# A two-layer transformer kernel on one core: scratch layout, pipeline distance and start-up order of its first attention are changed

## The chip, the core and the metric

The kernel runs on one core of a Trainium2 chip. Its time is the device time of one execution in microseconds (us). The engines are TensorE (PE, with its weight loads as PEld), VectorE (DVE), ScalarE (ACT), GpSimd (POOL) and SyncE (SP, here used to start transfers); each works through a queue of its own in the order written, and they signal one another with semaphores. 16 DMA engines move data.

## What is computed

Four blocks follow one another on x, 2 x 1024 rows of 128 numbers: an attention with 8 heads, a feed-forward net with ternary weights, a delta-rule attention, a feed-forward net with sign weights. Only the first block is touched by the change:

```
xn = layernorm(x) * gamma + beta
q, k = xn @ Wq + bq, xn @ Wk + bk        # 8 heads of 16 columns
v = xn @ Wv + bv                         # 8 heads of 128 columns
p = softmax(q @ k.T / 4)                 # per batch and head, 1024 x 1024
out = (p @ v).reshape(S, B, D, H).sum(-1)
x = layernorm(x + out)
```

The sum over the last axis adds up 8 neighbouring columns of v, so the kernel sums Wv and bv first, and each head needs 16 columns of v only.

## The kernel before, in words

Two batches of 8 heads are 16 heads, each with 8 tiles of 128 keys or queries.

**Start-up.** The 2048 rows come in four groups of 512 (`GROUPS`). Per group DVE takes statistics (L384), POOL forms the inverse deviation (L297), DVE normalises (L393), PE transposes (L470), ACT applies gamma and beta (L253), PE projects q, k and v (L483, L486, L493), and q and k are cut into a rounded part (ACT, L267, L269) and the rest (DVE, L404, L407). DVE sums Wv and bv (L423, L425) and adds bv to v (L415). `store_splits` (L176) writes the parts to two scratch tensors in DRAM, 3 planes x batch x 128 x 1024, the rounded part twice. `load_stacks` (L187) reads a head back as 48 rows: 3 planes of its 16 rows, each head twice (partitions 0 and 64) for q and for k, four transfers of 192 KB. There are 4 buffers for such stacks. SP does all of it in one order: stores of groups 0 and 1, stacks of head 0, stores of group 2, stacks of head 1, stores of group 3, stacks of head 2, then the ffn weights (L218 to L225, 10 transfers), and only then, head by head, `load_shift(h)` and `load_stacks(h + 3)`; the weights of the third block follow those of heads 0 and 1.

**Steps.** PE then runs through numbered steps (L540). Step s computes the raw scores of one query tile (`row_scores`, L503, L504: head s // 8), DVE takes their row maxima (L446). When a head's 8 maxima are there, POOL splits them (L315), PE transposes them into a row at step 8(h+1)+1 (`shift_step`, L512), ACT copies the row out (L279), and SP lays it into rows 48, 49, 112 and 113 of the head's q stack with four transfers (L203). From step 8(h+1)+5 on (`LAG` = 5, `score_step`) PE computes the transposed scores with the maximum already subtracted (L524), ACT exponentiates them (L285), and 2 steps later PE multiplies with v (L536). So in most steps PE has the row scores of one head, the scores of the head before it, and a product with v. A queue waits as a whole: where L524 of a new head waits for its shift rows, the row scores behind it wait too. At the end of a head DVE folds the result (L453) and POOL adds it to X. A stack buffer is free for head h + 4 when the scores of head h are done (L194). POOL also splits the ffn weights (heads 1 to 6), prepares convolution weights (heads 7 to 9) and masks (head 10).

Of the kernel before, what the change touches and what calls it, by code (L numbers as in the profile page):

```python
# [5 lines left out]
ALU = mybir.AluOpType  # L6
# [41 lines left out]
def build(nc, dr, out_dram):  # L48
    x_dram = dr["L0_attn_x"]
    q_scratch = nc.dram_tensor("q_scratch", (3, B, P, S), F32, kind="Internal").ap()  # L50
    k_scratch = nc.dram_tensor("k_scratch", (3, B, P, S), F32, kind="Internal").ap()

    with ExitStack() as ctx:
        program(nc, dr, out_dram, x_dram, q_scratch, k_scratch, ctx)


def program(nc, dr, out_dram, x_dram, q_scratch, k_scratch, ctx):
# [54 lines left out]
    LAG = 5  # L112
# [5 lines left out]
    wv_sum, bv_sum = sb("wv_sum", [P, P]), sb("bv_sum", [P, P])  # L118
# [5 lines left out]
    wv, bv_rows, ones_row = prob[:, 0, :], prob[:, 1, :], prob[0:2, 2, :]  # L124
# [3 lines left out]
    folded = sb("folded", [P, 2, 8, 32])  # L128
    rsum, att = sb("rsum", [P, 8]), sb("att", [P, 8, DK0])

    with nc.Block() as block:
        x_in = [sem(f"x_in{g}") for g in range(GROUPS)]
        weights_in, v_weights_in = sem("weights_in"), sem("v_weights_in")
# [4 lines left out]
        q_hi, k_hi, q_lo, k_lo, v_ready = sem("q_hi"), sem("k_hi"), sem("q_lo"), sem("k_lo"), sem("v_ready")  # L138
        splits_stored = [sem(f"splits_stored{g}") for g in range(GROUPS)]
# [6 lines left out]
        T_BANK, Q_BANK, K_BANK, V_BANK = 4, 5, 6, 7  # L146
# [7 lines left out]
        def shift_step(h):  # L154
            return 8 * (h + 1) + 1
# [15 lines left out]
        def _(sp):  # L171
# [46 lines left out]
            for o, name in ((W1, "w1"), (W2, "w2")):  # L218
                sp.dma_start(w_raw[:, o:o + FH], dr[f"L0_ffn_{name}_w"]).then_inc(w_in, 16)
            for o, name, n in ((WH1, "h1", FH), (WH2, "h2", FH), (W3, "w3", D)):  # L220
                sp.dma_start(w_raw[:, o:o + FB * n].rearrange("p (k n) -> p k n", k=FB),
                             dr[f"L0_ffn_{name}_w"].rearrange("(k p) n -> p k n", p=P)).then_inc(w_in, 16)
            for i, name in enumerate(("w1", "w2", "h1", "h2")):
                sp.dma_start(ffn_scale[:, i, :], dr[f"L0_ffn_{name}_s"]).then_inc(w_in, 16)
            sp.dma_start(w3s[:], dr["L0_ffn_w3_s"].rearrange("(p o) -> p o", o=1)).then_inc(w_in, 16)  # L225

            for h in range(NH):
# [3 lines left out]
                if h == 0:  # L231
# [3 lines left out]
                if h == 1:  # L235
# [7 lines left out]
        def _(act):  # L243
            for dst, src in ((gam, "gamma"), (bet, "beta"), (bq, "bq"), (bk, "bk")):
                act.dma_start(dst[:], dr["L0_attn_" + src].rearrange("(p o) -> p o", o=1)).then_inc(weights_in, 16)
            for dst, src in ((wq, "Wq"), (wk, "Wk")):
                act.dma_start(dst[:], dr["L0_attn_" + src]).then_inc(weights_in, 16)
# [14 lines left out]
            load_xnT(0)  # L262
            for g in range(GROUPS):
                if g >= 2:
                    act.wait_ge(splits_stored[g - 2], 4 * 16)
                act.wait_ge(q_psum, g + 1)
                nc.scalar.activation(qsp[:, g % 2, 0, :], ps[:, Q_BANK, :], ACT.Identity, bias=bq[:, 0:1]).then_inc(q_hi, 1)  # L267
                act.wait_ge(k_psum, g + 1)
                nc.scalar.activation(ksp[:, g % 2, 0, :], ps[:, K_BANK, :], ACT.Identity, bias=bk[:, 0:1]).then_inc(k_hi, 1)  # L269
                if g + 1 < GROUPS:  # L270
                    load_xnT(g + 1)

            for i, unit in enumerate(ring_order):
# [15 lines left out]
        def _(pool):  # L289
# [17 lines left out]
            nc.gpsimd.memset(vp[:, :, :, 16:17], 1.0).then_inc(ones_set, 1)  # L307
# [56 lines left out]
            for h in range(NH):  # L364
# [16 lines left out]
        def _(dve):  # L381
            link = Chain(dve, dve_step)

            def stats(g):  # L384
# [6 lines left out]
                last.then_inc(stats_ready, 1)  # L391
# [1399 lines left out]
```

## Time and profile before

| | us |
|---|---|
| median of 3 runs (816.42 to 827.82) | 824.22 |
| the profiled execution | 825.39 |
| its span, first to last instruction | 823.7 |
| PE, DVE, ACT, POOL busy | 615.6, 490.4, 284.6, 286.1 |
| mean granted TensorE clock | 0.784 of full |

The busy times are shares of the whole span, in which four blocks with different limits follow one another; they don't tell what bounds the first block. For that one reads its own stretches of time. The granted clock is that of TensorE alone; it has two levels, 1.2 and 2.4 GHz, shown as 0.50 and 1.00.

### The profile page before, as it was taken

The numbers are of one execution on the slowest core, as the hardware profiler recorded it, in microseconds if no ns is written. First come the engines' busy times: TensorE is split into PE (matmuls) and PEld (weight loads), VectorE is DVE, ScalarE is ACT, GpSimd is POOL, SyncE is SP. The second block draws the span as 40 slices with busy tenths as digits, with TensorE's granted clock in tenths as the row PEclk, the third lists the DMA queues.
The fourth block names the chain that finished last, engine by engine and source line by source line (L and its number), as shares of the span: only waits on it lengthen the run. The fifth ranks groups of instructions, "written<-read, shape, count | busy, mean of one in ns | idle before, by whom it ended". The sixth has DMA issues, their size and how long they took to land. (4 is left out here: it accounts for less than half of the span.)

```text
span 823.7 us, 16498 instructions
## 1 busy us (share of the span) xinstructions
PE 615.6 (75%) x6944; PEld 378.0 (46%) x6944; DVE 490.4 (60%) x790; ACT 284.6 (35%) x519; POOL 286.1 (35%) x385
## 2 busy tenths in 40 slices
PE   4440898988999896999998588859733489448884
PEld 2210333333333334777676366644423378335662
DVE  5460588678568524554545323347997897655773
ACT  2200566567457463243341144520100011214331
POOL 2100142324201012554455302489960002236673
PEclk9855689799558577999999889988956555558887
DMA  4645311111111000000000010102202000000000
GB/s 134 227 162 151 106 53 65 62 65 56 45 49 60 4 2 2 1 0 1 1 0 1 0 28 2 26 30 53 53 3 53 4 4 3 2 0 1 13 14 25
DMA packets 36910, 32.18 MB, mean 39 GB/s; under 512 B 21588, under 2 KB 28244, under 8 KB 36836
## 3 DMA queue, kind: packets, MB, share of 16 engines
q1 hardware_dynamic: 35684, 29.94, 12.0%
q10 hardware_dynamic: 1152, 1.18, 0.5%
q8 instruction: 55, 0.90, 0.5%
q14 instruction: 19, 0.16, 0.1%
HBM read 21.35 MB, written 9.44 MB: 37 GB/s over the span
## 5 line engine op out<-in xcount | busy, mean ns | idle before, releaser
L446 DVE TENSOR_REDUCE nmx<-ps 128x1 f32<-128x1024 f32 x128 | 154.6, 1221 | 100.3 <-PE ps L504 99.7
L285 ACT ACTIVATE prob<-ps 128x512 f32<-128x512 f32 x256 | 136.9, 596 | 109.0 <-PE ps L524 106.7
L524 PE MATMUL ps<-qst,kst 50*128 50x512 f32 x256 | 87.8, 600 | 41.8 <-DMA qst<-shift_sb 40.1
L536 PE MATMUL ps<-prob,vp 128*32 128x256 f32 x1024 | 99.3, 481 | 0.0
L633 POOL TENSOR_TENSOR h_lo<-hf,h_hi 128x512 fp32r<-128x512 f32 x48 | 63.7, 1338 | 69.6 <-DVE h_hi L663 69.6
L524 PEld LDWEIGHTS ps<-qst,kst 50*128 50x128 f32 x256 | 35.3, 223 | 107.3 <-ACT prob L285 46.3
L503 PE MATMUL ps<-kst,qst 48*128 48x512 f32 x128 | 67.4, 530 | 22.8 <-DMA kst<-k_scratch 18.9
L315 POOL CAST nsplit<-nmx 128x8 fp32r<-128x8 f32 x16 | 3.0, 190 | 214.7 <-DVE nmx L446 202.7
L504 PE MATMUL ps<-kst,qst 48*128 48x512 f32 x128 | 65.7, 516 | 0.0
L663 DVE CAST h_hi<-hf 128x512 fp32r<-128x512 f32 x48 | 41.8, 897 | 37.9 <-ACT hf L606 37.3
L707 PE MATMUL ps<-h_hi,w_lo 128*128 128x512 f32 x144 | 58.5, 406 | 7.7 <-issue 5.4
L1037 DVE SCALAR_TENSOR_TENSOR long_<-vpad,fir_l,long_ 128x1024 f32<-128x1024 f32 x46 | 59.0, 1285 | 1.5
L708 PE MATMUL ps<-h_lo,w_hi 128*128 128x512 f32 x144 | 57.0, 395 | 0.0
L709 PE MATMUL ps<-h_hi,w_hi 128*128 128x512 f32 x144 | 56.8, 395 | 0.0
L1663 POOL TENSOR_TENSOR h_lo<-hf,h_hi 128x512 fp32r<-128x512 f32 x32 | 43.7, 1390 | 23.4 <-DVE h_hi L1689 23.4
L536 PEld LDWEIGHTS ps<-prob,vp 128*32 128x32 f32 x1024 | 24.7, 122 | 55.3 <-issue 32.8
L503 PEld LDWEIGHTS ps<-kst,qst 48*128 48x128 f32 x128 | 31.3, 246 | 28.4 <-DMA kst<-k_scratch 19.6
L1689 DVE CAST h_hi<-hf 128x512 fp32r<-128x512 f32 x32 | 34.9, 1144 | 15.3 <-ACT hf L1633 15.0
L606 ACT ACTIVATE hf<-ps,ffn_scale 128x512 f32<-128x512 f32 x32 | 22.1, 690 | 59.1 <-PE ps L709 58.8
L707 PEld LDWEIGHTS ps<-h_hi,w_lo 128*128 128x128 f32 x144 | 27.0, 188 | 19.8 <-issue 8.7
L1227 POOL TENSOR_TENSOR vtok<-vtok,sq 128x512 f32<-128x512 f32 x4 | 5.1, 1263 | 86.6 <-DVE sq L1109 86.6
L504 PEld LDWEIGHTS ps<-kst,qst 48*128 48x128 f32 x128 | 31.6, 248 | 0.0
(236 smaller groups left out, 1187.4 us busy)
## 6 DMA issues: line engine op xcount, KB each, us to landing
qst<-q_scratch SPq DMA_DIRECT2D x32, 192.0 KB
kst<-k_scratch SPq DMA_DIRECT2D x32, 192.0 KB
q_scratch<-qsp SPq DMA_DIRECT2D x4, 512.0 KB, 3.3
k_scratch<-ksp SPq DMA_DIRECT2D x4, 512.0 KB, 4.4
w_raw<-L_ffn_h_w SPq DMA_DIRECT2D x2, 1024.0 KB, 13.2
X<-L_attn_x SPq DMA_DIRECT2D x4, 256.0 KB, 4.8
q_scratch<-qsp SPq DMA_DIRECT2D x4, 256.0 KB, 4.2
k_scratch<-ksp SPq DMA_DIRECT2D x4, 256.0 KB, 8.6
```

Source lines behind the costliest of these rows:

```text
L285: nc.scalar.activation(prob[:, n % PROBS, GT * half:GT * half + GT], ps[:, RINGB + i % RING, :], ACT.Exp, scale=SCORE_SCALE).then_inc(ring ...
L446: nc.vector.tensor_reduce(nmx[:, h % 2, k:k + 1], pair, AX.X, ALU.max, negate=True).then_inc(max_done, 1)
L503: nc.tensor.matmul(ps[:, bank, :], qst[0:48, p, P * k:P * k + P], kst[0:48, p, 0:GT], start=True, stop=True)
L504: nc.tensor.matmul(ps[:, bank + 1, :], qst[64:112, p, P * k:P * k + P], kst[64:112, p, GT:S], start=True, stop=True).then_inc(max_psum, 1)
L524: nc.tensor.matmul(ps[:, RINGB + i % RING, :], kst[r:r + 50, p, P * t:P * t + P], qst[r:r + 50, p, GT * half:GT * half + GT], start=True, ...
L536: last = nc.tensor.matmul(ps[32 * j:32 * j + 32, PVB, 0:256], vp[:, h, t, :], prob[:, n % PROBS, 256 * j:256 * j + 256], start=(t == 0), s ...
L633: nc.gpsimd.tensor_tensor(h_lo[:, layer % 2, o, :], hf[:, o, :], h_hi[:, layer % 2, o, :].bitcast(F32), ALU.subtract).then_inc(lo_ready, 1)
L707: nc.tensor.matmul(out, wl, xh, start=start, stop=False)
L708: nc.tensor.matmul(out, wh, xl, start=False, stop=False)
L709: return nc.tensor.matmul(out, wh, xh, start=False, stop=stop)
L1037: ins = nc.vector.scalar_tensor_tensor(long_[:, b], vpad[:, b, t:t + S], fir_l[:, t:t + 1], long_[:, b], ALU.mult, ALU.add)
L1663: nc.gpsimd.tensor_tensor(h_lo[:, layer, o, :], hf[:, o, :], h_hi[:, layer, o, :].bitcast(F32), ALU.subtract).then_inc(lo_ready, 1)
```

## The change

The scratch tensors become batch x 128 x 3 x 1024, so that the 48 rows of a head lie one behind the other, and the loads of a head read them as such. The rows of heads 0 and 1 (the first 32) are stored first. Stacks of heads 0 to 2 are loaded before the stores of groups 2 and 3. The shift goes in with two transfers rather than four and one step later (+2); the scores follow at +8 rather than +5, so 6 steps lie between the two rather than 4. The ffn weights are started after head 1's shift and stacks, those of the third block after heads 3 and 4, and POOL's work on them moves by three heads. In the start-up q and k of groups 0 and 1 get PSUM banks of their own, ACT copies v out, POOL sums Wv and bv by halves, bv enters by a matmul with a row of ones, DVE waits for the four small vectors first and adds the epsilon, and the projections of group 3 are done in steps 1 to 3. PE gets 12 extra matmuls at the start and 2 in each of the steps 5 to 17, whose results nobody reads.

```diff
-    q_scratch = nc.dram_tensor("q_scratch", (3, B, P, S), F32, kind="Internal").ap()
-    k_scratch = nc.dram_tensor("k_scratch", (3, B, P, S), F32, kind="Internal").ap()
+    q_scratch = nc.dram_tensor("q_scratch", (B, P, 3, S), F32, kind="Internal").ap()
+    k_scratch = nc.dram_tensor("k_scratch", (B, P, 3, S), F32, kind="Internal").ap()
...
-    LAG = 5
+    LAG = 8
...
-T_BANK, Q_BANK, K_BANK, V_BANK = 4, 5, 6, 7
+T_BANK, V_BANK = 4, 7
+Q_BANK, K_BANK = (0, 2, 5, 5), (1, 3, 6, 6)
+EARLY = 2 * DK0
...
-    return 8 * (h + 1) + 1
+    return 8 * (h + 1) + 2
...
-    def store_splits(g):
+    def store_rows(g, rows, done):
         b, cols = g // 2, slice(GT * (g % 2), GT * (g % 2) + GT)
-        q_rows = q_scratch[:, b, :, cols].rearrange("a p t -> p a t")
-        k_rows = k_scratch[:, b, :, cols].rearrange("a p t -> p a t")
...
         sp.wait_ge(q_lo, g + 1)
-        sp.dma_start(q_rows[:, 0:2], qsp[:, g % 2].bitcast(F32)).then_inc(splits_stored[g], 16)
-        sp.dma_start(q_rows[:, 2:3], qsp[:, g % 2, 0:1].bitcast(F32)).then_inc(splits_stored[g], 16)
+        sp.dma_start(q_rows[:, 0:2], qsp[rows, g % 2].bitcast(F32)).then_inc(done, 16)
+        sp.dma_start(q_rows[:, 2:3], qsp[rows, g % 2, 0:1].bitcast(F32)).then_inc(done, 16)
         sp.wait_ge(k_lo, g + 1)
-        sp.dma_start(k_rows[:, 1:3], ksp[:, g % 2].bitcast(F32)).then_inc(splits_stored[g], 16)
-        sp.dma_start(k_rows[:, 0:1], ksp[:, g % 2, 0:1].bitcast(F32)).then_inc(splits_stored[g], 16)
+        sp.dma_start(k_rows[:, 1:3], ksp[rows, g % 2].bitcast(F32)).then_inc(done, 16)
+        sp.dma_start(k_rows[:, 0:1], ksp[rows, g % 2, 0:1].bitcast(F32)).then_inc(done, 16)
...
-        if h % 8 == 0:
+        if h == 0:
+            sp.wait_ge(first_rows_stored, 2 * 4 * 16)
+        if h == 2 or h == 8:
             sp.wait_ge(splits_stored[2 * b], 4 * 16)
             sp.wait_ge(splits_stored[2 * b + 1], 4 * 16)
...
-            sp.dma_start(qst[r:r + 48, p, :].bitcast(F32), q_scratch[:, b, rows, :]).then_inc(stack_in[p], 16)
-            sp.dma_start(kst[r:r + 48, p, :].bitcast(F32), k_scratch[:, b, rows, :]).then_inc(stack_in[p], 16)
+            sp.dma_start(qst[r:r + 48, p, :].bitcast(F32), q_scratch[b, rows].rearrange("e a t -> (e a) t")).then_inc(stack_in[p], 16)
+            sp.dma_start(kst[r:r + 48, p, :].bitcast(F32), k_scratch[b, rows].rearrange("e a t -> (e a) t")).then_inc(stack_in[p], 16)

     def load_shift(h):
         sp.wait_ge(ring_done, ring["shift", h] + 1)
         for r in (48, 112):
-            for j in range(2):
-                sp.dma_start(qst[r + j:r + j + 1, h % STACKS, :].bitcast(F32),
-                             shift_sb[8 * j:8 * j + 8, h % 2, :].bitcast(F32)).then_inc(shift_in, 16)
...
+            sp.dma_start(qst[r:r + 2, h % STACKS, :].bitcast(F32), shift_sb[:, h % 2, :].bitcast(F32)).then_inc(shift_in, 16)
+
+    sp.dma_start(wv, dr["L0_attn_Wv"]).then_inc(v_weights_in, 16)
+    sp.dma_start(bv_row, dr["L0_attn_bv"].rearrange("(o n) -> o n", o=1)).then_inc(v_weights_in, 16)
...
-    store_splits(0)
-    store_splits(1)
+    early_rows, other_rows, all_rows = slice(0, EARLY), slice(EARLY, P), slice(0, P)
+    store_rows(0, early_rows, first_rows_stored)
+    store_rows(1, early_rows, first_rows_stored)
     load_stacks(0)
-    store_splits(2)
+    store_rows(0, other_rows, splits_stored[0])
+    store_rows(1, other_rows, splits_stored[1])
     load_stacks(1)
-    store_splits(3)
     load_stacks(2)
-
...
+    store_rows(2, all_rows, splits_stored[2])
+    store_rows(3, all_rows, splits_stored[3])
+
+    def load_ffn_weights():
...
-        if h == 0:
+        if h == 1:
+            load_ffn_weights()
+        if h == 3:
...
-        if h == 1:
+        if h == 4:
...
-    act.dma_start(wv, dr["L0_attn_Wv"]).then_inc(v_weights_in, 16)
-    act.dma_start(bv_rows, dr["L0_attn_bv"].rearrange("(o n) -> o n", o=1).broadcast_to([P, H0 * D])).then_inc(v_weights_in, 16)
+        act.dma_start(dst[:], dr["L0_attn_" + src]).then_inc(qk_weights_in, 16)
...
-    act.wait_ge(weights_in, 6 * 16)
+    act.wait_ge(ln_weights_in, 4 * 16)
...
+    def leading_q(g):
         if g >= 2:
             act.wait_ge(splits_stored[g - 2], 4 * 16)
+            act.wait_ge(first_rows_stored, 2 * 4 * 16)
         act.wait_ge(q_psum, g + 1)
-        nc.scalar.activation(qsp[:, g % 2, 0, :], ps[:, Q_BANK, :], ACT.Identity, bias=bq[:, 0:1]).then_inc(q_hi, 1)
+        nc.scalar.activation(qsp[:, g % 2, 0, :], ps[:, Q_BANK[g], :], ACT.Identity, bias=bq[:, 0:1]).then_inc(q_hi, 1)
+
+    def leading_k(g):
         act.wait_ge(k_psum, g + 1)
-        nc.scalar.activation(ksp[:, g % 2, 0, :], ps[:, K_BANK, :], ACT.Identity, bias=bk[:, 0:1]).then_inc(k_hi, 1)
-        if g + 1 < GROUPS:
-            load_xnT(g + 1)
+        nc.scalar.activation(ksp[:, g % 2, 0, :], ps[:, K_BANK[g], :], ACT.Identity, bias=bk[:, 0:1]).then_inc(k_hi, 1)
...
+    def values(g):
+        b, half = g // 2, g % 2
+        act.wait_ge(v_psum, g + 1)
+        nc.scalar.copy(vp[:, 8 * b:8 * b + 8, 4 * half:4 * half + 4, 0:DK0],
+                       ps[:, V_BANK, :].rearrange("p (t h e) -> p h t e", t=4, e=DK0)).then_inc(v_ready, 1)
+
+    load_xnT(0)
+    leading_q(0)
+    load_xnT(1)
+    leading_k(0)
+    leading_q(1)
+    leading_k(1)
+    values(0)
+    load_xnT(2)
+    values(1)
+    load_xnT(3)
+    leading_q(2)
+    leading_k(2)
+    values(2)
+    leading_q(3)
+    leading_k(3)
+    values(3)
...
-        link(nc.gpsimd.tensor_scalar(rs[:, g, :], mv[:, g, :, 1], LN_EPS, None, ALU.add))
...
+    pool.wait_ge(v_weights_in, 2 * 16)
+    for src, dst in ((wv, wv_sum), (bv_row, bv_sum)):
+        n8 = src.rearrange("p (n e) -> p n e", e=H0)
+        link(nc.gpsimd.tensor_tensor(n8[:, :, 0:4], n8[:, :, 0:4], n8[:, :, 4:8], ALU.add))
+        link(nc.gpsimd.tensor_tensor(n8[:, :, 0:2], n8[:, :, 0:2], n8[:, :, 2:4], ALU.add))
+        nc.gpsimd.tensor_tensor(dst[:].rearrange("p (n o) -> p n o", o=1), n8[:, :, 0:1], n8[:, :, 1:2], ALU.add).then_inc(wv_summed, 1)
...
-        if 1 <= h < 7:
-            if h == 1:
+        if 4 <= h < 10:
+            if h == 4:
                 pool.wait_ge(w_in, 16 * W_LOADS)
-            for i in range(2 * h - 2, min(2 * h, WSPLITS)):
+            for i in range(2 * h - 8, min(2 * h - 6, WSPLITS)):
                 split_weights(i)
-        if 7 <= h < 10:
-            convolve_weights(h - 7)
-        if h == 10:
+        if 10 <= h < 13:
+            convolve_weights(h - 10)
+        if h == 13:
             make_masks()
...
-        last.then_inc(stats_ready, 1)
+        link(last)
+        nc.vector.tensor_scalar(rs[:, g, :], mv[:, g, :, 1], LN_EPS, None, ALU.add).then_inc(stats_ready, 1)
...
+    dve.wait_ge(ln_weights_in, 4 * 16)
     stats(0)
     stats(1)
     normalise(0)
-    dve.wait_ge(v_weights_in, 2 * 16)
-    nc.vector.tensor_reduce(wv_sum[:], wv.rearrange("p (n e) -> p n e", e=H0), AX.X, ALU.add).then_inc(wv_summed, 1)
     normalise(1)
-    nc.vector.tensor_reduce(bv_sum[:], bv_rows.rearrange("p (n e) -> p n e", e=H0), AX.X, ALU.add).then_inc(wv_summed, 1)
     stats(2)
-    left_over(0)
+    rest_q(0)
+    rest_k(0)
     stats(3)
+    rest_q(1)
+    rest_k(1)
     normalise(2)
-    dve.wait_ge(wv_summed, 2)
-    values(0)
-    left_over(1)
     normalise(3)
-    values(1)
-    left_over(2)
-    values(2)
-    left_over(3)
-    values(3)
+    rest_q(2)
+    rest_k(2)
...
+        if step == 3:
+            rest_q(3)
+            rest_k(3)
...
+    def warm(columns, count):
+        for _ in range(count):
+            nc.tensor.matmul(ps[:, V_BANK, 0:P], columns, ident[:], start=True, stop=True)
...
+    def project_q(g):
+        if g == 0:
+            pe.wait_ge(qk_weights_in, 2 * 16)
+        pe.wait_ge(xnT_ready, g + 1)
+        if g == 3:
+            pe.wait_ge(q_lo, g)
+        nc.tensor.matmul(ps[:, Q_BANK[g], :], wq[:], xnT[:, g % 2, :], start=True, stop=True).then_inc(q_psum, 1)
+
+    def project_k(g):
+        if g == 3:
+            pe.wait_ge(k_lo, g)
+        nc.tensor.matmul(ps[:, K_BANK[g], :], wk[:], xnT[:, g % 2, :], start=True, stop=True).then_inc(k_psum, 1)
...
+    def project_v(g):
+        if g == 0:
+            pe.wait_ge(wv_summed, 2)
+            pe.wait_ge(ones_set, 2)
+        else:
+            pe.wait_ge(v_ready, g)
+        for n in range(4):
+            out = ps[:, V_BANK, P * n:P * n + P]
+            nc.tensor.matmul(out, xnT[:, g % 2, P * n:P * n + P], wv_sum[:], start=True, stop=False)
+            last = nc.tensor.matmul(out, one[:], bv_sum[:], start=False, stop=True)
+        last.then_inc(v_psum, 1)
+
+    warm(ident[:], 12)
     transposes(0)
...
+    project_q(0)
+    transposes(1)
+    project_k(0)
+    project_q(1)
+    project_k(1)
+    project_v(0)
+    transposes(2)
+    project_v(1)
+    project_q(2)
+    project_k(2)
+    transposes(3)
+    project_v(2)
...
+        if step == 0:
+            pe.wait_ge(q_lo, 2)
+            pe.wait_ge(k_lo, 2)
...
+        if step == 1:
+            project_q(3)
+        if step == 2:
+            project_k(3)
+        if step == 3:
+            project_v(3)
+        if step == 5:
+            pe.wait_ge(v_ready, GROUPS)
+        if 5 <= step < shift_step(0) + LAG:
+            for _ in range(2):
+                nc.tensor.matmul(ps[:, PVB, 256:256 + P], wq[:], ident[:], start=True, stop=True)
```

## Rows read from the trace of the kernel before

**Rows 1.** Windows by stage: busy us (and instructions) per engine, clock, DMA share, GB/s.

```profile
43.07:82.92 39.85, 9.90 (x27) 3.69 (x28) 14.89 (x13) 0.26 (x1) 0.39 (x2) 0.50 0.52 159
82.92:313.46 230.54, 209.11 (x1525) 78.99 (x1525) 148.09 (x146) 140.26 (x271) 53.10 (x119) 0.77 0.15 51
```

**Rows 2.** Timeline of the start-up: start us, duration us, engine, line, instruction, idle before.

```profile
10.74 2.08 PE L483 MATMUL ps<-xnT,wq 128*128 128x512 f32 x2 [1.21 <-ACT xnT L258]
...
22.66 0.75 DVE L407 SCALAR_TENSOR_TENSOR ksp<-ps,bk,ksp 128x512 fp32r<-128x512 f32 x1
...
23.20 1.02 PE L483 MATMUL ps<-xnT,wq 128*128 128x512 f32 x2
...
24.59 0.71 SPq L185 DMA_DIRECT2D k_scratch<-ksp  x1
...
29.32 0.76 SPq L196 DMA_DIRECT2D qst<-q_scratch  x1
...
43.08 0.79 PE L503 MATMUL ps<-kst,qst 48*128 48x512 f32 x1 [13.67 <-DMA kst<-k_scratch]
...
43.91 9.14 DVE L446 TENSOR_REDUCE nmx<-ps 128x1 f32<-128x1024 f32 x8 [11.73 <-PE ps L504]
```

**Rows 3.** Windows, columns as in rows 1: group stores; ffn weights; stack loads alone.

```profile
21.62:25.03 3.41, 3.19 (x17) 1.97 (x16) 3.41 (x13) 1.90 (x3) 2.35 (x5) 1.00 0.96 354
...
62.58:72.82 10.24, 0.00 (x0) 0.00 (x0) 0.89 (x1) 0.00 (x0) 0.00 (x0) 0.50 0.87 227
243.49:246.90 3.41, 3.41 (x17) 1.36 (x17) 2.10 (x5) 1.67 (x4) 0.00 (x0) 0.50 0.20 67
```

**Rows 4.** Timeline: head 0's shift row copied, and SP's last weight transfer.

```profile
58.45 0.26 ACT L279 CAST shift_sb<-ps 16x128 fp32r<-16x128 f32 x1 [27.92 <-PE ps L512]
...
76.56 0.69 SPq L225 DMA_DIRECT2D w3s<-L_ffn_w_s  x1
```

**Rows 5.** Waits: engine, line, what it waited for: us in total, times, longest.

```profile
PE ps L524 <- DMA qst<-shift_sb: 40.1, 12, 20.9
```

**Rows 6.** Timeline of two shifts, behind a stack load and without one.

```profile
191.95 0.73 SPq L196 DMA_DIRECT2D qst<-q_scratch  x1
...
200.28 2.71 SPq L203 DMA_DIRECT2D qst<-shift_sb  x4
...
206.62 0.50 PE L524 MATMUL ps<-qst,kst 50*128 50x512 f32 x2 [2.73 <-DMA qst<-shift_sb]
...
252.82 2.71 SPq L203 DMA_DIRECT2D qst<-shift_sb  x4
...
256.71 0.49 PE L524 MATMUL ps<-qst,kst 50*128 50x512 f32 x2 [0.49 <-DMA qst<-shift_sb]
```

**Rows 7.** Windows, columns as in rows 1: a shift wait, and what followed.

```profile
202.53:205.94 3.41, 1.36 (x16) 0.46 (x12) 2.05 (x2) 1.52 (x3) 0.95 (x1) 1.00 0.20 66
...
209.36:250.31 40.95, 40.95 (x228) 14.66 (x222) 24.65 (x25) 20.12 (x39) 6.93 (x31) 0.50 0.13 47
```

**Rows 8.** Timeline of SP: shifts of neighbouring heads, at full and at half clock.

```profile
110.03 2.70 SPq L203 DMA_DIRECT2D qst<-shift_sb  x4
...
121.06 2.71 SPq L203 DMA_DIRECT2D qst<-shift_sb  x4
...
217.31 2.71 SPq L203 DMA_DIRECT2D qst<-shift_sb  x4
...
235.08 2.71 SPq L203 DMA_DIRECT2D qst<-shift_sb  x4
```

**Rows 9.** Timeline of PE: first and last scores of the last head.

```profile
302.67 0.49 PE L524 MATMUL ps<-qst,kst 50*128 50x512 f32 x2 [0.23 <-DMA qst<-shift_sb]
...
310.64 0.68 PE L524 MATMUL ps<-qst,kst 50*128 50x512 f32 x2
```

**Rows 10.** DMA issues: transfer, queue, count, KB, us to landing.

```profile
bk<-L_attn_bk ACTq DMA_DIRECT2D x1, 0.5 KB, 4.9
```

**Rows 11.** Timeline of PE: the v projection of a group, 4 matmuls in 8 records.

```profile
25.37 1.13 PE L493 MATMUL ps<-wv_sum,xnT 128*128 128x128 f32 x8
```

More of the change, by code:

```diff
@@ L128, in program @@
     folded = sb("folded", [P, 2, 8, 32])
+    one = sb("one", [1, P])
     rsum, att = sb("rsum", [P, 8]), sb("att", [P, 8, DK0])
@@ L208, in _ @@
                 sp.dma_start(kst[r:r + 2, :, :].bitcast(F32), ones_row.rearrange("p (o t) -> p o t", o=1).broadcast_to([2, STACKS, S])).then_inc(ones_in, 16)
-            store_splits(0)
-            store_splits(1)
+            early_rows, other_rows, all_rows = slice(0, EARLY), slice(EARLY, P), slice(0, P)
+            store_rows(0, early_rows, first_rows_stored)
+            store_rows(1, early_rows, first_rows_stored)
             load_stacks(0)
-            store_splits(2)
+            store_rows(0, other_rows, splits_stored[0])
+            store_rows(1, other_rows, splits_stored[1])
             load_stacks(1)
-            store_splits(3)
             load_stacks(2)
[L218 to L225, printed above, removed]
+            store_rows(2, all_rows, splits_stored[2])
+            store_rows(3, all_rows, splits_stored[3])
+            def load_ffn_weights():
+                for o, name in ((W1, "w1"), (W2, "w2")):
+                    sp.dma_start(w_raw[:, o:o + FH], dr[f"L0_ffn_{name}_w"]).then_inc(w_in, 16)
+                for o, name, n in ((WH1, "h1", FH), (WH2, "h2", FH), (W3, "w3", D)):
+                    sp.dma_start(w_raw[:, o:o + FB * n].rearrange("p (k n) -> p k n", k=FB),
+                                 dr[f"L0_ffn_{name}_w"].rearrange("(k p) n -> p k n", p=P)).then_inc(w_in, 16)
+                for i, name in enumerate(("w1", "w2", "h1", "h2")):
+                    sp.dma_start(ffn_scale[:, i, :], dr[f"L0_ffn_{name}_s"]).then_inc(w_in, 16)
+                sp.dma_start(w3s[:], dr["L0_ffn_w3_s"].rearrange("(p o) -> p o", o=1)).then_inc(w_in, 16)
             for h in range(NH):
@@ L295, in _ @@
             link(nc.gpsimd.memset(neg_half[:], -0.5))
+            nc.gpsimd.memset(one[:], 1.0).then_inc(ones_set, 1)
             def rstd(g):
                 pool.wait_ge(stats_ready, g + 1)
-                link(nc.gpsimd.tensor_scalar(rs[:, g, :], mv[:, g, :, 1], LN_EPS, None, ALU.add))
                 nc.gpsimd.tensor_tensor(rs[:, g, :], rs[:, g, :], neg_half[:, 0:4], ALU.pow).then_inc(rstd_ready, 1)
@@ L400, in normalise, with rest_q, rest_k @@
                 last.then_inc(xn_ready, 1)
-            def left_over(g):
+            def rest_q(g):
                 dve.wait_ge(q_hi, g + 1)
-                nc.vector.scalar_tensor_tensor(qsp[:, g % 2, 1, :], ps[:, Q_BANK, :], bq[:, 0:1], qsp[:, g % 2, 0, :].bitcast(F32),
+                nc.vector.scalar_tensor_tensor(qsp[:, g % 2, 1, :], ps[:, Q_BANK[g], :], bq[:, 0:1], qsp[:, g % 2, 0, :].bitcast(F32),
                                                ALU.add, ALU.subtract).then_inc(q_lo, 1)
+            def rest_k(g):
                 dve.wait_ge(k_hi, g + 1)
-                nc.vector.scalar_tensor_tensor(ksp[:, g % 2, 1, :], ps[:, K_BANK, :], bk[:, 0:1], ksp[:, g % 2, 0, :].bitcast(F32),
+                nc.vector.scalar_tensor_tensor(ksp[:, g % 2, 1, :], ps[:, K_BANK[g], :], bk[:, 0:1], ksp[:, g % 2, 0, :].bitcast(F32),
                                                ALU.add, ALU.subtract).then_inc(k_lo, 1)
-            def values(g):
-                b, half = g // 2, g % 2
-                dve.wait_ge(v_psum, g + 1)
-                heads = vp[:, 8 * b:8 * b + 8, 4 * half:4 * half + 4, 0:16].rearrange("p h t e -> p t h e")
-                for t in range(4):
-                    last = nc.vector.tensor_tensor(heads[:, t], ps[:, V_BANK, 128 * t:128 * t + 128].rearrange("p (h e) -> p h e", e=16),
-                                                   bv_sum[:].rearrange("p (h e) -> p h e", e=16), ALU.add)
-                last.then_inc(v_ready, 1)
+            dve.wait_ge(ln_weights_in, 4 * 16)
             stats(0)
@@ L476, in transposes @@
                 last.then_inc(xnT_psum, 1)
-            transposes(0)
-            for g in range(GROUPS):
+            def project_q(g):
+                if g == 0:
+                    pe.wait_ge(qk_weights_in, 2 * 16)
                 pe.wait_ge(xnT_ready, g + 1)
-                if g >= 1:
+                if g == 3:
                     pe.wait_ge(q_lo, g)
-                nc.tensor.matmul(ps[:, Q_BANK, :], wq[:], xnT[:, g % 2, :], start=True, stop=True).then_inc(q_psum, 1)
-                if g >= 1:
+                nc.tensor.matmul(ps[:, Q_BANK[g], :], wq[:], xnT[:, g % 2, :], start=True, stop=True).then_inc(q_psum, 1)
+            def project_k(g):
+                if g == 3:
                     pe.wait_ge(k_lo, g)
-                nc.tensor.matmul(ps[:, K_BANK, :], wk[:], xnT[:, g % 2, :], start=True, stop=True).then_inc(k_psum, 1)
-                if g + 1 < GROUPS:
-                    transposes(g + 1)
-                pe.wait_ge(wv_summed, 2)
-                if g >= 1:
+                nc.tensor.matmul(ps[:, K_BANK[g], :], wk[:], xnT[:, g % 2, :], start=True, stop=True).then_inc(k_psum, 1)
[4 more added lines that the diff above has]
+                else:
                     pe.wait_ge(v_ready, g)
                 for n in range(4):
-                    last = nc.tensor.matmul(ps[:, V_BANK, P * n:P * n + P], xnT[:, g % 2, P * n:P * n + P], wv_sum[:], start=True, stop=True)
+                    out = ps[:, V_BANK, P * n:P * n + P]
+                    nc.tensor.matmul(out, xnT[:, g % 2, P * n:P * n + P], wv_sum[:], start=True, stop=False)
+                    last = nc.tensor.matmul(out, one[:], bv_sum[:], start=False, stop=True)
                 last.then_inc(v_psum, 1)
+            warm(ident[:], 12)
+            transposes(0)
+            project_q(0)
[10 more added lines that the diff above has]
+            project_v(2)
             def row_scores(h, k):
```

22 lines of the change are left out of this document (10 added, 12 removed).

## The prediction

> **What bounds the kernel now.** I read the windows by stage first, then the timeline of what ends the waits in each. Nothing of the change reaches past the first attention, which ends at 313.46 us [rows 1], so the other 510 us are carried over as they are. The attention has two stretches. Until 82.92 almost nothing runs: between 43.07 and 82.92 PE is busy 9.90 of 39.85 us [rows 1]. From 82.92 on PE is busy 209 of 230.5 us, against 148 for DVE, 140 for ACT and 53 for POOL [rows 1]. So PE bounds the second stretch, but at a mean clock of 0.77, and not without holes.
>
> Three things stand behind these numbers, and the reader should see each in its row.
>
> *Narrow loads.* While only stacks are loaded, the DMA engines are busy 0.20 of the time and move 67 GB/s; group stores and ffn weights reach shares of 0.96 and 0.87, and 354 and 227 GB/s [rows 3]. 0.20 is about 3 of 16 engines, and the source of a stack load has 3 planes as its outermost dimension where the stores have 128 rows. A head's four transfers (0.79 MB) take 0.79/67 = 11.7 us at that rate; the first row scores wait 13.8 us from the first issue of head 0's load, 29.32 to 43.08 [rows 2].
>
> *Late shifts.* Head 0's shift row is copied at 58.45, but SP starts its last weight transfer at 76.56 and only then turns to it [rows 4]: the longest wait, 20.9 us. The other 11 waits for shift rows sum to 40.1 - 20.9 = 19.2 us [rows 5]. With no stack load ahead, a shift needs 3.9 us from first issue to scores (252.82 to 256.71); behind one it needs 6.3 (200.28 to 206.62, with the stack load issued from 191.95 on) [rows 6].
>
> *Low clock.* A stretch with such a wait, PE busy 1.36 of 3.41 us, is followed by 41 us at 0.50 (1.2 GHz), with PE recorded busy throughout, 40.95 of 40.95 [rows 7]. A head takes 121.06 - 110.03 = 11.03 us at full clock and 235.08 - 217.31 = 17.77 us at half [rows 8], so each us at half clock costs 1 - 11.03/17.77 = 0.38 us. A mean of 0.77 over 230.5 us is 2 x 0.23 x 230.5 = 106 us at half, a loss of 40 us.
>
> Check: step 13 to step 127 is 114 steps of 11.03/8 = 1.38 us, or 157; then 15 steps at the pace of the last head's scores, (310.64 - 302.67)/7 = 1.14 [rows 9], or 17; 157 + 17 + 19 + 40 = 233, against 230.5 recorded.
>
> **The start-up, to the first row maxima.** DVE now waits for four small vectors, the last of which needs 4.9 us to land [rows 10] and is there some 7 us in, about 3 us after DVE started before. Against that, PE no longer waits between projections for DVE, sums of Wv are POOL's (two trees of three small additions, done by about 16 us, before PE asks for them), and values are ACT's. What counts is the last split of group 1, 23.41 us before [rows 2]. Four projections of q and k at 2 us each (early pace) or 1 (later pace) [rows 2] set it: 20 to 25; I take 22. Then: stores of 32 rows, two k issues and landing, 4 us (before, with 128 rows, 4.7 from 24.59 to 29.32 [rows 2]), so head 0's loads are issued from 26; four issues of 0.73 to 29; four stores of the other rows, 2.4, and 4 to land, 35.3; these gate ACT's rounded q of group 2, whose buffer they empty; with three operations of 0.75 the DVE queue gets to its first maximum at 37.6, against 43.91 [rows 2]. The stacks themselves are there by 32: at 227 to 354 GB/s they need 2.2 to 3.5 us rather than 11.7. Heads 1 and 2 are loaded behind this and have 8 and 16 steps of cover.
>
> **Steps 0 to 15.** Their floor is DVE's 9.14/8 = 1.14 us per maximum [rows 2], 18.3 us. Group 3's projections now stand in steps 1 to 3: q and k 2 us each at half clock, v twice a group's 1.13 [rows 11] because of the ones row, 4.5 at half; 8.5 in all, about 6 beyond what DVE hides (2 at full clock). The two extra matmuls per step cost 0.28 each (1.13/4), 0.56 at half; DVE's maximum covers them at full clock, at half the cover is gone for about 0.4 us a step, and six such steps give 2.5. The 12 at the start fill time in which PE has nothing. First scores at 37.6 + 18.3 + 6 + 2.5 = 64.4 (57 to 70), against 82.92. Head 0's shift is ready at step 10 and has six steps; no weights stand in front of it.
>
> **The pipeline after it.** 111 steps of 1.38 lead to step 127: 153 us. Moving scores from +5 to +8 lengthens the tail to 18 steps of 1.14, 20.5 us, and 0.5 for the last fold: end at 238.4 if the clock stays up and nothing waits, 75 us before 313.46. Of that 75, about 18.5 is the earlier start, 19 the shift waits, 40 the low clock; the three later steps give back 3.
>
> The shift waits go for three reasons: stack loads leave the queues within about 3.5 us, the shift has two issues (1.35 us) instead of four (2.71), and six steps (8.3 us) between its transpose and its use instead of four. One margin shrinks: stacks of head h + 3 are now issued at step 8h + 15 and needed at 8h + 24, 9 steps rather than 12, 12.4 us; issue and landing need 2.9 + about 2, and SP is free again 0.9 us before the next shift. POOL's weight work moves by three heads; with 53 us of work in 230 it stays far from the path, and a shift split queues behind one head's share at most, which the two extra steps cover.
>
> The ffn weights now stand on SP between head 4's stacks and head 2's shift. 5632 columns x 128 x 4 bytes are 2.88 MB: 8.1 to 12.7 us at 354 to 227 GB/s [rows 3]. Shift 2 adds 2.5 to be issued and land: 10.6 to 15.2, against 12.4 - 2.9 = 9.5 us of cover. PE waits 1 to 6 us there; I take 3. The later block's weights (1 MB, heads 3 and 4) stay within the cover.
>
> The clock is what I can't compute. It will be low at the first steps, where PE has had nothing to do; one low stretch of the trace lasts 41 us with PE busy throughout [rows 7], and the wait at head 2 can begin another. Between none and two such stretches I take half of one, 21 us at half beyond step 16: 8 us.
>
> **Sum.** Span 823.7 - 75 + 3 + 8 = 759.7; the profiled execution took 825.39, 1.7 more than its span and 1.2 above the median. Forecast: 761 us. Its own range: 746 to 778.
>
> **Rivals.** About 2% (16.5 us: 807.7 and 840.7) is what a measurement tells from no change.
>
> *The clock comes back at once,* and no wait takes it down: 761 - 8 = 753. For it: the loss of the clock in [rows 7] follows a wait of PE, and these go. Against it: the 41 us in the second of those rows. The Trainium skill, "TensorE: Matmul & The Clock Gate", Part 1, says that sustained matmul work releases the clock soon, and that only idleness takes it back; the first half of that disagrees with the 41 us of [rows 7], the second agrees. By that rule the result would be this rival's.
>
> *Long low stretches stay,* about 100 us as now, begun by the start-up or the weights wait: 761 + (100 - 21) x 0.38 = 791.
>
> *The loads stay narrow,* that is, the layout does not do what it is for: then a load needs 11.7 + 2 us against 12.4 of cover, the next shift stands behind it as before, the stores of the other rows land behind head 0's stacks and the maxima start at 44 as before, first scores at 71, and the pipeline keeps its 230.5 + 3: end at 305, 820 in all with the weights wait. Against it: the 128-row transfers of [rows 3]. The Trainium skill, "DMA: Bandwidth & Descriptors", section on why a DMA increments its semaphore by 16, says that the number of engines is the largest divisor, up to 16, common to both sides' outermost dimensions. By it a stack load goes from 3 to 16 engines, as 0.20 agrees for the 3; by it a shift transfer, 2 rows outermost, goes onto 2 engines. No row shows that; a late shift would show it.
>
> *Slower:* in the first steps the clock stays low and never returns, since a stream at half clock already feeds on itself for 41 us in [rows 7]. Step pace 2.22, tail 1.84 a step: first scores 67, 111 x 2.22 = 247, tail 33, end at 347, 859 in all. It decides for slower only once over (840.7 - 753)/0.38 = 231 of those 280 us are at half; before it was 106 of 230.
>
> **Chances.** Forecast 0.62, clock at once 0.12, long low stretches 0.14, narrow loads 0.07, low throughout 0.03, something unseen 0.02. Faster 0.90, within 2% 0.07, slower 0.03. The range goes from 743 (first scores at 57, no half clock, 1 us at the weights) to 795 (first scores at 70, 75 us at half, 6 us at the weights, and most of the third case).
>
> **What would show it.** Stack loads at a DMA share near 0.9 for some 3 us; first row maxima near 38 and first scores near 64; shift waits gone but for one of 1 to 6 us at head 2; heads 11.0 us apart; last fold near 249; a mean clock over 0.9 in the pipeline. The prediction is wrong if the shift waits remain, if PE stays at half for over 75 us, or if another engine sets the pace of a head.

## The result, and the profile after

The changed kernel takes 769.2 us (median of 4 runs, 758.2 to 778.8) against 826.0 for the kernel before: 0.926 of it, 95% interval 0.907 to 0.945. The forecast was 761 with a range of 743 to 795. The profiled execution took 765.9 us, its span is 764.2. All ratios and intervals here compare only the fast executions of both kernels (those within about 1.5% of their kernel's fastest), while the medians are over all of them, so that a ratio is not the quotient of two medians.

The windows by stage and of single events, with the columns of [rows 1], cut at the first scores (72.46) and the last fold (257.59), which stood at 82.92 and 313.46:

```profile
38.84:72.46 33.62, 33.62 (x98) 19.62 (x97) 20.47 (x18) 2.80 (x5) 0.39 (x2) 0.50 0.55 150
72.46:257.59 185.13, 174.49 (x1528) 67.47 (x1527) 144.64 (x144) 139.91 (x271) 53.82 (x119) 0.94 0.34 75
101.30:108.20 6.90, 2.10 (x12) 0.70 (x12) 0.83 (x1) 1.09 (x2) 0.00 (x0) 0.65 0.69 137
108.20:253.50 145.30, 141.84 (x1297) 54.34 (x1293) 123.14 (x124) 118.44 (x230) 51.79 (x111) 0.99 0.31 64
150.60:152.40 1.80, 1.80 (x22) 0.67 (x16) 1.79 (x2) 1.65 (x4) 0.40 (x2) 1.00 0.64 184
150.28:153.50 3.22, 3.22 (x36) 1.14 (x34) 3.17 (x4) 2.91 (x6) 0.40 (x2) 1.00 0.71 163
257.59:764.17 506.58, 376.32 (x5328) 282.66 (x5328) 309.19 (x558) 134.46 (x234) 223.82 (x244) 0.81 0.06 13
```

The pipeline lasts 185 us where it lasted 230.5. DVE and ACT do the same work as in [rows 1]; what shrinks is PE's idle time, from 21.4 to 10.6 us, and its time at half clock: the mean clock went from 0.77 to 0.94. From 108 to 253 us the clock is 0.99 of full and PE is busy 142 of 145 us. While SP issues a stack load (fifth row), the DMA share is now 0.64 at 184 GB/s, and over 3.2 us from the first issue (sixth row) 0.71 at 163 GB/s, where [rows 3] had 0.20 and 67; the forecast was a share near 0.9.

The waits of PE for shift rows (columns of [rows 5]); there were 12 of 40.1 us:

```profile
PE ps L581 <- DMA qst<-shift_sb: 6.4, 1, 6.4
```

Its place, in the timeline of SP and PE:

```profile
88.16 0.31 SPq L201 DMA_DIRECT2D qst<-q_scratch  x1
...
89.92 0.90 SPq L228 DMA_DIRECT2D w_raw<-L_ffn_w_w  x2
...
92.63 3.93 SPq L233 DMA_DIRECT2D ffn_scale<-L_ffn_w_s  x2
...
97.95 1.47 SPq L234 DMA_DIRECT2D w3s<-L_ffn_w_s  x1
99.46 1.27 SPq L207 DMA_DIRECT2D qst<-shift_sb  x2
...
106.10 0.79 PE L581 MATMUL ps<-qst,kst 50*128 50x512 f32 x2 [6.42 <-DMA qst<-shift_sb]
```

Head 4's stacks, ffn weights, and then head 2's shift: SP gets to the shift 9.5 us after the first weight transfer, and its rows are there another 6.6 us later, behind the 2.88 MB. The start-up, to be held against [rows 2]:

```profile
28.52 0.80 PE L534 MATMUL ps<-wv_sum,xnT 128*128 128x128 f32 x2
29.24 0.79 PE L535 MATMUL ps<-bv_sum,one 1*128 1x128 f32 x2
...
35.48 0.39 PE L534 MATMUL ps<-wv_sum,xnT 128*128 128x128 f32 x2
...
35.68 0.78 ACT L267 ACTIVATE xnT<-ps,bet,gam 128x512 f32<-128x512 f32 x1 [3.58 <-PE ps L510]
36.36 0.68 ACT L276 ACTIVATE qsp<-ps,bq 128x512 fp32r<-128x512 f32 x1
...
38.84 0.79 PE L560 MATMUL ps<-kst,qst 48*128 48x512 f32 x1
...
39.67 2.36 DVE L474 TENSOR_REDUCE nmx<-ps 128x1 f32<-128x1024 f32 x2 [1.19 <-PE ps L561]
```

And two of the steps 5 to 15, in PE's timeline, with the shifts of neighbouring heads later on, in SP's:

```profile
65.70 1.22 PE L620 MATMUL ps<-ident,wq 128*128 128x128 f32 x4
66.85 0.79 PE L560 MATMUL ps<-kst,qst 48*128 48x512 f32 x1
...
67.58 1.22 PE L620 MATMUL ps<-ident,wq 128*128 128x128 f32 x4
```

```profile
155.20 1.27 SPq L207 DMA_DIRECT2D qst<-shift_sb  x2
...
165.97 1.27 SPq L207 DMA_DIRECT2D qst<-shift_sb  x2
```

A step lasts 67.58 - 65.70 = 1.88 us there, and the first row maximum is at 39.67. A head takes 165.97 - 155.20 = 10.77 us at full clock.

### The profile page after: what moved, and what is told of

The parts are those of the page before. It is cut to its first block and busy times, and to the rows that moved or that the text cites. A ratio compares the mean times of both kernels' runs of the same rounds, so it can differ in the third digit from the quotient of the medians.

```text
span 764.2 us, 16680 instructions
## 1 busy us (share of the span) xinstructions
PE 614.1 (80%) x7052; PEld 389.6 (51%) x7052; DVE 491.6 (64%) x776; ACT 286.6 (38%) x523; POOL 290.7 (38%) x388
## 5 line engine op out<-in xcount | busy, mean ns | idle before, releaser
L581 PE MATMUL ps<-qst,kst 50*128 50x512 f32 x256 | 75.3, 516 | 10.0 <-DMA qst<-shift_sb 6.4
L593 PE MATMUL ps<-prob,vp 128*32 128x256 f32 x1024 | 80.8, 401 | 0.0
L581 PEld LDWEIGHTS ps<-qst,kst 50*128 50x128 f32 x256 | 28.7, 189 | 65.6 <-ACT prob L317 43.6
L560 PE MATMUL ps<-kst,qst 48*128 48x512 f32 x128 | 59.6, 468 | 0.0
L561 PE MATMUL ps<-kst,qst 48*128 48x512 f32 x128 | 58.1, 457 | 0.0
L593 PEld LDWEIGHTS ps<-prob,vp 128*32 128x32 f32 x1024 | 22.2, 110 | 44.1 <-ACT prob L317 32.0
L1758 DVE CAST h_hi<-hf 128x512 fp32r<-128x512 f32 x32 | 35.0, 1145 | 13.9 <-ACT hf L1702 13.1
L1702 ACT ACTIVATE hf<-ps,s_out 128x512 f32<-128x512 f32 x32 | 20.7, 689 | 29.4 <-PE ps L1814 18.6
L778 PEld LDWEIGHTS ps<-h_hi,w_hi 128*128 128x128 f32 x144 | 27.0, 188 | 6.6
```

The source lines that it names most:

```text
L560: nc.tensor.matmul(ps[:, bank, :], qst[0:48, p, P * k:P * k + P], kst[0:48, p, 0:GT], start=True, stop=True)
L561: nc.tensor.matmul(ps[:, bank + 1, :], qst[64:112, p, P * k:P * k + P], kst[64:112, p, GT:S], start=True, stop=True).then_inc(max_psum, 1)
L581: nc.tensor.matmul(ps[:, RINGB + i % RING, :], kst[r:r + 50, p, P * t:P * t + P], qst[r:r + 50, p, GT * half:GT * half + GT], start=True, ...
L593: last = nc.tensor.matmul(ps[32 * j:32 * j + 32, PVB, 0:256], vp[:, h, t, :], prob[:, n % PROBS, 256 * j:256 * j + 256], start=(t == 0), s ...
L778: return nc.tensor.matmul(out, wh, xh, start=False, stop=stop)
```

## Experiments

The open questions: which part of the change brings the gain, whether narrow loads, late shifts and low clock are one chain, and what the new wait and the slow first steps cost. The theory: the width of the stack loads is nearly all of it. The rival: distance, order and start-up carry a good part. Medians of this table come from 4 to 6 runs (7 or 11 for the kernel before); first scores, last fold, waits and half clock are of the one profiled execution of each (half clock from first scores to last fold, from the granted clock).

| kernel | median us | ratio to before (95%) | first scores | last fold | shift waits us | at half us |
|---|---|---|---|---|---|---|
| before | 824 to 833 | 1 | 82.9 | 313.5 | 40.1 | 108 |
| changed | 769.2 | 0.926 (0.907 to 0.945) | 72.5 | 257.6 | 6.4 | 21 |
| layout only | 755.5 | 0.916 (0.910 to 0.922) | 60.7 | 250.5 | 16.0 | 38 |
| changed, old layout | 819.9 | 0.980 (0.970 to 0.990) | 76.7 | 326.3 | 24.0 | 150 |
| changed, weights early | 758.0 | 0.917 (0.910 to 0.924) | 72.2 | 248.0 | 0 | 11 |
| changed, no extra matmuls | 765.3 | 0.925 (0.917 to 0.933) | 64.0 | 251.7 | 6.1 | 33 |
| changed, old distance | 766.4 | 0.937 (0.924 to 0.949) | 67.9 | 264.4 | 9.3 | 43 |
| both repairs | 747.5 | 0.916 (0.910 to 0.923) | 62.4 | 235.6 | 4.7 | 9 |
| all, weights spread | 749.9 | 0.914 (0.906 to 0.923) | 58.2 | 233.6 | 0 | 13 |
| layout and spread | 743.2 | 0.912 (0.904 to 0.920) | 50.7 | 233.5 | 5.9 | 20 |
| the same, two transfers | 743.0 | 0.902 (0.890 to 0.913) | 50.0 | 229.6 | 0.2 | 26 |

The kernel before was run beside each group of kernels, at 827.0, 824.8 and 833.2 us. The rows stand by group: layout only to no extra matmuls; old distance, both repairs, layout and spread; the other two.

**Layout only.**

```diff
-q_scratch = nc.dram_tensor("q_scratch", (3, B, P, S), ...)
+q_scratch = nc.dram_tensor("q_scratch", (B, P, 3, S), ...)
-sp.dma_start(qst[r:r + 48, p, :]..., q_scratch[:, b, rows, :])
+sp.dma_start(qst[r:r + 48, p, :]..., q_scratch[b, rows].rearrange("e a t -> (e a) t"))
```

(The same for k, and for the views that the stores write through.)

> The kernel before with the new scratch layout and the loads that read it, nothing else. Theory (the width of the stack loads is the cause of nearly all of it): a stack load lasts about 3 us on all DMA engines, row maxima begin near 34 us, SP is through with the ffn weights near 60, first scores at 62 to 66 instead of 82.9; a shift needs 3.9 us and has four steps of 1.38, so the 11 short shift waits go and with them most of the half clock; 755 to 775 us. Rival (distance, order and start-up carry a good part): shift waits of 1 to 3 us stay at the heads, 785 to 805 us.

755.5 us: the layout alone gives the whole gain. Its median is 14 us below that of the full change, but the two intervals, 0.910 to 0.922 and 0.907 to 0.945, overlap: that it is faster is not shown. Windows of it, the start-up's DMA (stores of group 3 and stacks together) and the pipeline's last 154 us; then its waits, all and between 96 and 250 us; then head 0's shift:

```profile
36.00:40.00 4.00, 2.43 (x8) 0.86 (x6) 4.00 (x4) 0.00 (x0) 0.00 (x0) 0.50 1.07 326
...
96.30:249.90 153.60, 146.12 (x1335) 57.86 (x1335) 125.44 (x127) 121.09 (x235) 44.23 (x105) 0.99 0.28 56
```

```profile
PE ps L524 <- DMA qst<-shift_sb: 16.0, 14, 11.5
...
PE ps L524 <- DMA qst<-shift_sb: 4.6, 13, 1.0
```

```profile
46.28 0.26 ACT L279 CAST shift_sb<-ps 16x128 fp32r<-16x128 f32 x1 [16.32 <-PE ps L512]
...
53.93 2.72 SPq L203 DMA_DIRECT2D qst<-shift_sb  x4
...
60.69 0.79 PE L524 MATMUL ps<-qst,kst 50*128 50x512 f32 x2 [11.45 <-DMA qst<-shift_sb]
```

With the old distance and four transfers, 13 shifts cost 4.6 us (0.35 each, at most 1.0) instead of 19.2 us in 11, and once the clock has risen at 98.4 it stays until after the last fold. Head 0's shift still waits behind the block of weights: its row is there at 46.54, and SP turns to it at 53.93. The first row maximum comes at 35.85, against 43.91 in the kernel before and 39.67 in the changed one.

**Changed, old layout.** The layout's edit undone, all others kept.

> The changed kernel with the old scratch layout (three planes outermost) and all its other edits. Theory: DMA share near 0.2 while stacks load, a load of 11.7 us, shift waits of 1 to 4 us at most heads and low clock after them, 805 to 825 us. Rival (the greater distance and the two transfers are enough): few waits, at most 785 us.

As the theory said, 819.9; at 0.970 to 0.990, the other edits without the layout bring 1 to 3%. What the theory had not said: the greater distance does take most of the waits away, 4 are left. Windows at one of them and behind it:

```profile
144.09:150.91 6.82, 1.61 (x20) 0.46 (x12) 2.29 (x2) 1.76 (x4) 0.39 (x2) 0.80 0.22 74
154.33:195.28 40.95, 40.95 (x219) 14.22 (x222) 23.77 (x25) 20.80 (x41) 11.82 (x20) 0.50 0.13 47
```

Of PE's 150 us at half clock here, 20 lie before the first wait; the other 130 are four stretches, one begun at each of the four waits (13.1, 6.2, 2.2 and 2.5 us long). The profiled execution, 837 us, is longer than the kernel's median. So a wait of a few us costs itself and then the low stretch behind it: the one of these windows lasts from 148.1 to 199.3, the one of [rows 7] from 208.0 to 252.3. The short waits are another matter: no wait of the kernel before under 1.9 us, and none of the 13 of the layout alone behind 96 us, the longest of 1.0, is followed by a fall of the clock, while in the kernel before five of the six from 1.96 to 3.4 us are. The first row maximum is at 44.64 here, no earlier than the 43.91 of before.

**Changed, weights early.** `load_ffn_weights()` stands before the loop over heads, as in the kernel before.

> The changed kernel with the ffn weights started before head 0's shift again, as in the kernel before. Theory (the move is not needed once stack loads are fast, and costs a wait at head 2): SP is through with them near 62, just before shift 0 is ready at 63; the wait of 6.4 us at head 2 and the 7 us of half clock around it go: 7 to 9 us less, 755 to 763 us. Rival (they delay shift 0): first scores 5 to 20 us later, 770 to 790 us.

No shift wait is left and the last fold comes 9.5 us earlier; the median, 758.0 us, is 11 below that of the changed kernel, though the intervals overlap. With wide loads SP is through with the weights at 58.2, before shift 0 is ready at 63.2. By the profiles the move of the weights was a cost, not a gain.

**Changed, no extra matmuls.**

```diff
-if 5 <= step < shift_step(0) + LAG:
-    for _ in range(2):
-        nc.tensor.matmul(ps[:, PVB, 256:256 + P], wq[:], ident[:], start=True, stop=True)
```

> The changed kernel without the two extra matmuls in steps 5 to 17 (the 12 at the start stay). Theory (they are on the path at half clock): these steps take 1.14 us instead of 1.87, first scores near 64 instead of 72.5, 757 to 764 us. Rival (they bring the clock back early and are worth their cost): first scores near 64, but PE stays at half 20 to 40 us longer, 768 to 778 us.

The row maxima behind group 3's projections, in DVE's timeline:

```profile
51.95 14.80 DVE L474 TENSOR_REDUCE nmx<-ps 128x1 f32<-128x1024 f32 x13 [3.97 <-PE ps L561]
```

They follow one another without a gap at 14.80/13 = 1.14 us, though PE is at half clock, and first scores come at 64.0, as expected, 8.5 us earlier. The total, 765.3, is just above the expected 757 to 764, and its interval overlaps that of the changed kernel: in the profiled execution the wait at head 2 brought 24 us at half instead of 7. Alone, this run settles the cost of the extra matmuls in their steps, not in the total. Nothing shows that they bring the clock back: PE is at full clock 8.9 us after first scores without them (at 72.9) and 13.8 with them (at 86.3); with the weights early it is 8.7 without (both repairs) and 11.3 with. In the other kernels without them it is 9 to 38.

**Changed, old distance.** `LAG` = 5, shift at +1, four transfers.

> The changed kernel with the distance of before (shift at +1, scores at +5) and four shift transfers again. Theory (with wide stack loads a shift needs 3.9 us and four steps of 1.38 hold it nearly): first scores after 13 steps, some 6 us earlier, short waits of at most 1 us per head, 4 to 6 us in all; about the same as the changed kernel, 760 to 772 us, the one long wait now at head 1 or 2, where the ffn weights stand. Rival (the greater distance is needed): waits of 1 to 3 us at each head and low clock after them, 780 to 800 us.

766.4 us, inside the theory's 760 to 772. First scores come 4.6 us earlier; 13 waits cost 9.3 us rather than the expected 4 to 6, 5.5 of it at the weights, where 34 us at half clock begin. Six steps or four is worth nothing that this can measure.

**Both repairs.** Weights early and no extra matmuls.

> The changed kernel with the ffn weights back in their old place and without the extra matmuls in steps 5 to 17: both repairs at once. Theory (both costs are on the path and add): first scores near 64, no wait at head 2, last fold at 238 to 246, 745 to 756 us. Rival (without the extra matmuls the clock stays low longer): last fold at 248 to 256, 757 to 766 us.

747.5 us, last fold at 235.6, before the expected 238 to 246: 22 us earlier than in the changed kernel, where the two repairs alone gave 9.5 and 5.9, so the two costs add. Some 2 us of the rest are chance: up to the first row maximum the code is that of the changed kernel, and the maximum came at 37.72 here, at 39.34 to 39.67 with the one repair, the other or none. A wait of 4.7 us stays at head 0: its shift row is copied by 52.7 now, and SP is at the weights until 57.1. **No bias rows** is the same, but leaves bv out, and so computes another result:

> As the run with both repairs, and bv left out (the matmul with the row of ones is not issued), to price it. Theory (group 1's and 2's v projections at half clock hold up the last rounded parts, and so the first row maximum): first maximum at 34 to 37 us instead of 39.6. Rival (the stores of the other rows set it, as I had predicted): it stays within 0.5 us of 39.6.

One run, 744.2 us. The first maximum is at 36.30, against 37.72 with both repairs. ACT's rounded q of group 2 is released by the landing of the stores in either, first with both repairs, then without bias rows:

```profile
35.68 0.69 ACT L276 ACTIVATE qsp<-ps,bq 128x512 fp32r<-128x512 f32 x1 [0.75 <-DMA k_scratch<-ksp]
...
34.26 0.69 ACT L276 ACTIVATE qsp<-ps,bq 128x512 fp32r<-128x512 f32 x1 [4.53 <-DMA k_scratch<-ksp]
```

So the stores are the gate that I had predicted, in both, and the 1.4 us between the two are a difference in when the stores landed: they don't price the ones row, and the theory of this run, that PE's v projections held up the rounded parts, is not shown by it. In the profiled execution of the changed kernel PE did come last.

**Layout and spread.** The kernel before, new layout, and the ffn weights behind the stacks of heads 0 to 3:

```diff
 load_stacks(h + 3)
+load_ffn_weights(h)   # h = 0: w1, w2; 1: h1; 2: h2; 3: w3 and the scales
```

> The kernel before with the new layout, and its ffn weights spread over heads 0 to 3, one or two transfers behind each head's stacks (POOL's splits three heads later, as in the changed kernel). Theory (the weights in one block were the 11.5 us wait at head 0 of the run with the layout alone): first scores near 50 instead of 60.7, no wait over 1.5 us, last fold at 236 to 244, 742 to 754 us. Rival (each part of the weights delays the next shift instead, or the low clock lasts as much longer): 755 to 765 us.

743.2 us, first scores at 50.7, last fold at 233.5 (expected 236 to 244): the best so far, and none of the start-up's reordering is in it. The first row maximum is at 35.96. **All, weights spread** is the changed kernel without its extra matmuls and with this spread:

> The changed kernel without the extra matmuls in steps 5 to 17 and with the ffn weights spread over heads 0 to 3. Theory (the start-up order, the stores and the distance bring little of their own): first scores near 58, some 7 us later than in the kernel with the layout and the spread weights alone, but no shift waits: last fold at 229 to 236, 738 to 750 us, within 1% of that one. Rival (order and distance are worth something once the waits are gone): 5 to 10 us faster than it, 733 to 738 us.

749.9: first scores 7.6 us later, no waits, the same last fold (233.6 against 233.5). The first row maximum is at 38.39, 2.4 us later, for all the reordering before it. The rest of the change is worth nothing here. What each part of the reordered start-up does alone (the early stores, the banks, the matmul for bv) was not tested. **The same, two transfers** puts the shift's two transfers into the kernel with layout and spread:

> The kernel with the new layout and the spread weights, and the shift in two transfers instead of four, at the old distance. Theory (half the issue time, 1.3 us less before the shift has landed): the 15 waits of 5.9 us in all go to under 1 us, 739 to 744 us. Rival (a transfer of two rows lands later, being carried by fewer DMA engines): waits as long or longer, 743 to 750 us.

The waits go from 5.9 us to 0.2, so a transfer of two rows does not land late enough to be waited for; the total, 743.0, does not move by what can be measured. The two kernels ran in different groups; 733.3 to 748.9 and 741.5 to 749.7 overlap.

## Why the prediction was right, point by point

*Loads.* Right, and shown both ways: the layout alone gives 0.916, all the rest without it 0.980. The Trainium skill, "DMA: Bandwidth & Descriptors", section on why a DMA increments its semaphore by 16, would give 3 engines for three planes outermost and 16 for 48 rows; the 0.20 of [rows 3] and the 0.22 above agree with the first, and the shares of 0.64 and 0.71 with more than 3. Its 2 engines for the new shift transfers may hold, but cost nothing that shows.

*Late shifts.* Right for the 11 waits. The wait at head 2 was predicted at 1 to 6 us, taken as 3, and is 6.4. The term that was short is landing: the shift's rows need 6.6 us from first issue behind the weights, not the 2.5 taken from a queue without them.

*Pipeline.* From first scores to last fold 174 + 3 + 8 = 185 us were forecast and 185.1 measured. That is partly luck. The wait was 3.4 us longer than taken, and a head took 10.77 us rather than 11.03, which gives back 3.6 over the 111 steps. Half clock was taken as 21 us there and is 21, but between 9 and 43 in the experiments with wide loads: the 21 was a middle.

*Clock.* The rival in which it comes back at once (753) did not come: PE was at half from 38.5 to 86.3. The step behind the forecast, that the clock falls where PE waits, holds for the fall at head 2 (103.4, in the wait of 6.4 us). It is not the whole: in the start-up the clock fell at 38.5 with no wait of PE before it (rows at the end). With this fall the sentence that only idleness takes the clock back, which the prediction found borne out by [rows 7], does not agree.

*Steps 0 to 15.* Here the prediction failed: first scores at 72.5, outside the 57 to 70 given. The step that failed is "at half the cover is gone for about 0.4 us a step, and six such steps give 2.5". The price of the two matmuls was right: 1.15 us from start to start (65.70 to 66.85), where 1.12 was taken. But with the row scores' 0.73 behind them (66.85 to 67.58) a step of PE is 1.88 us, 0.74 above DVE's 1.14 rather than 0.4; the 0.79 of a row score at half clock in [rows 2] would have given 0.79 + 1.12 - 1.14 = 0.77. And PE stayed at half in all 11 of these steps before the first scores, not in six: 8.1 us in place of 2.5. The rest of the term held: without the extra matmuls 37.6 + 18.3 + 6 = 61.9 would have been the forecast, and first scores came at 64.0, late by the 2 us by which the maxima began late.

*First maxima.* 39.67 rather than 37.6. The gate was taken to be the stores, and in two of the experiments it is, with the maximum at 37.72 and 36.30. In the changed kernel's profiled execution PE came last: DVE had waited 1.19 us for the row scores, which started at 38.84 behind group 2's v projection (from 35.48). ACT's rounded q of group 2 (36.36) was late too, behind the group 3 copy (35.68), which waited for PE. Both stood behind group 1's v matmuls at half clock, where the matmul of the ones row takes 0.79 us, as much as one of 128 rows (0.80). The earlier start itself, 43.91 to 37.6 in the forecast, is the layout's: the kernel with the layout alone has its first maximum at 35.85, the one with everything but the layout at 44.64. By these runs the reordering of the start-up gained nothing.

*Sum.* The span is 764.2 against 759.7: +2.1 for the first maxima, +6.0 for the steps, 0 for the pipeline, -3.7 in the three later blocks, which the change does not touch and whose clock varies by itself. The median is 8 us above the forecast.

The prediction gave 18.5 us of the gain to the earlier start. It was 10.5 (82.9 to 72.5), and it comes from the layout as well: with the layout alone first scores are at 60.7.

## What to carry to other kernels

Look at the DMA share while one kind of transfer runs alone: a small fixed fraction says that it uses few engines, and the order of its dimensions in DRAM is then worth more than its place in the schedule. A wait of TensorE can cost several times its length through the low clock behind it, as those of 2 us and more mostly did here and those of up to 1 us did not, so look at the longest waits first, and place bulk loads in pieces where every urgent transfer has room behind them. Matmuls meant to fill idle time must be priced at half clock, and with cover that is there at half clock.

## What the runs showed of the hardware that I had not expected

SP's issue of a transfer gets long when others are queued: the two small transfers of `ffn_scale` (2 KB each) take 3.93 us to issue behind the 2.88 MB, and 0.96 us when the weights are spread; a stack transfer is issued in 0.42 us instead of 0.73 though it is of the same size. In the changed kernel PE was at 1.2 GHz from 38.5 to 86.3 us, recorded busy in 47.80 of 47.80 us, and rose 13.8 us after the first scores; in the kernel with the layout alone it took 37.7 us after them. Nor did that stretch begin with a wait. Two windows before it, and its own:

```profile
31.00:35.10 4.10, 4.10 (x7) 1.70 (x7) 0.00 (x0) 0.59 (x1) 0.00 (x0) 0.50 1.05 405
35.10:38.50 3.40, 3.40 (x20) 2.55 (x19) 1.41 (x2) 1.93 (x3) 0.00 (x0) 1.00 1.00 283
38.50:86.30 47.80, 47.80 (x164) 25.95 (x163) 27.61 (x24) 9.43 (x18) 0.79 (x4) 0.50 0.39 108
```

PE is recorded busy throughout, rises to full clock at 35.1 and falls again at 38.5. What in the work begins and ends a low stretch stays open: in the pipeline of the kernel before alone they last from 3.4 to 44 us, and up to 51 with the old layout, with the same instructions.
